# A four-stage sandwich on one core: weight loads issued in the first block, the convolution written a group ahead, gate and router products moved into the norm blocks, bias loops with transposes a group ahead

## The reference, cut to what matters

```python
x = x + ln(conv_attention_mixture(ln(x)))   # stage a
x = x + ln(fp4_experts(ln(x)))              # stage b
x = x + ln(linear_attention(ln(x)))         # stage c
x = x + ln(windowed_transformer(ln(x)))     # stage d, six layers
# stage a
y = xp[:, 0:T]*w_dw[:, 0] + xp[:, 1:T+1]*w_dw[:, 1] + xp[:, 2:T+2]*w_dw[:, 2]
x = x + einsum('btd,ed->bte', y, w_pw)
...                                          # causal linear attention, then
h = ln(x)*ln_g + ln_b
gw = softmax(einsum('btd,ed->bte', h, w_moe_gate))       # 4 experts
ffn = sum_e gw_e * (silu(h @ w1_e.T + b1_e) @ w2_e.T + b2_e)
# stage b
logits = x @ router_w.T                                  # 16 experts, the best 2 kept
out = sum_e combine_e * (expert_e(x) + bias_down_e)
```

## Time and profile before

| what | value |
|---|---|
| median of 3 runs | 5442.13 us (5440.97 to 5442.73) |
| the profiled execution | 5434.87 us, its span 5433.2 us |
| busy: PE, DVE, ACT, POOL | 89%, 74%, 70%, 45% of the span |
| mean granted clock of TensorE | 0.94 of 2.4 GHz |
| blocks from the start to `al` | 94.85 us |
| from the end of `al` to `ax` | 87.88 us |
| from the end of `ax` to `be` | 107.94 us |
| stage d and the output | 4103.20 us |

### The profile page before, as it was taken

How to read it: one execution, slowest core, us unless ns; L and a number is a source line. 1 busy time by engine, 2 the same in 40 slices (tenths; PEclk the granted TensorE clock), 3 DMA queues, 4 the chain that set the end, 5 groups by cost and what they waited for, 6 DMA issues and landing times. The chain is left out here.

```text
span 5433.2 us, 144088 instructions
## 1 busy us (share of the span) xinstructions
PE 4847.8 (89%) x42260; PEld 4060.2 (75%) x42260; DVE 4003.2 (74%) x11109; ACT 3810.0 (70%) x12437; POOL 2451.6 (45%) x3763
## 2 busy tenths in 40 slices
PE   5988949994299998999989998899989999799994
PEld 3657949984188876888778887788867888688883
DVE  5664757777588876888768887788867888688875
ACT  1334423431199986999869997799968999599982
POOL 0000000000466663666546664566636666366661
PEclk7997959997699998999999999999999999999997
DMA  0001100000111111111111111111111111111111
GB/s 21 2 17 39 39 1 0 0 0 4 49 27 27 27 49 27 27 27 27 51 28 27 27 27 47 29 27 27 27 50 28 27 27 27 51 24 27 27 49 31
DMA packets 103390, 149.33 MB, mean 27 GB/s; under 512 B 65245, under 2 KB 72690, under 8 KB 102386
## 3 DMA queue, kind: packets, MB, share of 16 engines
q1 hardware_dynamic: 93410, 107.27, 8.7%
q0 software_dynamic: 9232, 33.12, 1.9%
HBM read 49.13 MB, written 2.10 MB: 9 GB/s over the span
## 5 line engine op out<-in xcount | busy, mean ns | idle before, releaser
L2023 ACT ACTIVATE d_probs<-d_S_ps,d_neg_max 128x96 f32<-128x96 f32 x3072 | 1000.6, 342 | 13.5 <-DVE d_neg_max L2237 3.8
L1626 POOL TENSOR_TENSOR d_qk<-d_qk,d_sin_terms 128x512 f32<-128x512 f32 x768 | 960.8, 1272 | 29.7 <-DVE d_sin_terms L2209 29.7
L1801 PEld LDWEIGHTS d_S_ps<-d_kT,d_q_blocks 128*128 128x128 f32 x6144 | 791.8, 193 | 2.3
L1801 PE MATMUL d_S_ps<-d_kT,d_q_blocks 128*128 128x96 f32 x6144 | 791.1, 272 | 0.0
L2209 DVE TENSOR_TENSOR d_qk<-d_A_ps,d_tables 128x512 f32<-128x512 f32 x768 | 527.6, 687 | 229.0 <-ACT d_squares L1979 162.6
L2023 ACT ACTIVATION_READ_ACCUMULATOR d_probs<-d_S_ps,d_neg_max 128x1 f32 x3072 | 639.3, 208 | 0.0
L1758 PE MATMUL d_A_ps<-d_wqkv_hi,d_xT_hi 128*128 128x512 f32 x1152 | 556.2, 483 | 22.1 <-DVE d_sin_terms L2209 17.4
L1979 ACT ACTIVATE d_squares<-d_A_ps 128x512 f32<-128x512 f32 x768 | 462.6, 602 | 123.9 <-PE d_A_ps L1760 123.5
L2209 DVE TENSOR_TENSOR d_sin_terms<-d_A_ps,d_tables 128x512 f32<-128x512 f32 x768 | 522.8, 681 | 0.0
L1765 PE MATMUL d_T_ps<-d_ident,d_qk 128*128 128x128 f32 x3072 | 483.9, 281 | 36.5 <-POOL d_qk L1663 32.8
L2031 ACT ACTIVATE d_probsT<-d_PT_ps 96x512 f32<-96x512 f32 (+1 forms) x768 | 459.9, 599 | 79.8 <-PE d_PT_ps L1811 79.6
(11 more groups left out here) (406 smaller groups left out, 10766.6 us busy)
## 6 DMA issues: line engine op xcount, KB each, us to landing
d_v_early<-d_v SPq DMA_DIRECT2D x192, 256.0 KB, 3.0
d_v_early<-d_v SPq DMA_DIRECT2D x192, 128.0 KB, 2.3
d_tables<-L_ffn_rotary POOLq DMA_DIRECT2D x7, 2048.0 KB, 8.3
d_qk<-L_ffn_Wqkv POOLq DMA_DIRECT2D x21, 512.0 KB, 3.9
d_xs<-d_xb SPq DMA_DIRECT2D x56, 127.0 KB
d_xs<-d_xb SPq DMA_DIRECT2D x96, 63.5 KB
ax_fp_blocks<-L_ffn_blocks_gu SPq DMA_DIRECT2D x16, 256.0 KB, 3.7
ax_fp_scales<-L_ffn_scales_gu SPq DMA_DIRECT2D x64, 64.0 KB, 3.0
```

Of the source, the lines that this page charges most:

```text
L1626: nc.gpsimd.tensor_tensor(c4[:, :, s, :], c4[:, :, s, :], s4[:, :, 1 - s, :], ALU.add).then_inc(rotated, 1)
L1801: last = nc.tensor.matmul(S[g % 2][:, n * SEEN:(n + 1) * SEEN], qx[:, p, half, :], kT[b][jj][:, p, HALF * half:HALF * half + SEEN], start= ...
L2023: nc.scalar.activation(pr[:, g, n, seen_columns(g)], S[g % 2][:, n * SEEN:(n + 1) * SEEN], ACT.Exp, bias=nmax[:, g, n:n + 1], accum_out=de ...
```

## The change

- The first block and the block of six loads are gone. A function `load` runs on SP inside the `an` norm: x in eight transfers (a quarter of both halves each, with a semaphore for each quarter), then the identity, the ten weights of `av` and the six arrays of the gate and experts. DVE waits for a quarter ahead of each 8 tiles of statistics. The loads of `bt` are issued inside the norm `bn`.
- ACT copies a whole group of 4 transposed tiles in one instruction in all four norms.
- In `ao` and `bn` PE computes the logits of group g-1 behind the transposes of group g.
- `av` is written out without a loop. ACT makes the first tap, DVE the other two, one group ahead of the additions.
- In `as` and `bt` PE transposes group g+1 ahead of the product of group g. In `as` the softmax comes first, and the high and low parts are made between the groups of the loop. In `bt` DVE does the copy to y in ACT's place, and the high and low parts go into the loop in eighths.

The loads and the norm:

```diff
+            def load(sp):
+                x4 = x[:].rearrange("p (j b) d -> p j b d", b=B)
+                for q in range(4):
+                    js = slice(4 * q, 4 * q + 4)
+                    for b in range(B):
+                        sp.dma_start(x4[:, js, b, :], x_from[b].rearrange("(j p) d -> p j d", p=P)[:, js, :]).then_inc(x_in[q], DMA)
+                sp.dma_start(ident[:], ident_from).then_inc(ident_in, DMA)
...
             for n in range(N_TILES):
+                if arrived is not None:
+                    v.wait_ge(arrived[n // 8], 2 * DMA)
                 nc.vector.bn_stats(stats[:, n, :], x[:, n, :]).then_inc(stat, 1)
...
+            def project(g):
+                out, weight, columns, done = logits
+                pe.wait_ge(T_out, g + 1)
+                for t in range(G4):
+                    n = G4 * g + t
+                    last = nc.tensor.matmul(out[:, n * columns:(n + 1) * columns], xT(g)[:, t, :], weight, start=True, stop=True)
+                last.then_inc(done, 1)
...
                 last.then_inc(T_ps, 1)
+                if logits is not None and g:
+                    project(g - 1)
+            if logits is not None:
+                project(GROUPS - 1)
```

The convolution:

```diff
+                    for g in range(GROUPS):
+                        if g >= 2:
+                            act.wait_ge(t_ps, g - 1)
+                        nc.scalar.activation(cv[:, g % 2], taken(g, 0), ACT.Identity, scale=wdw[:, 0:1]).then_inc(tap, 1)
...
+                    def convolve(g):
+                        v.wait_ge(tap, g + 1)
+                        for k in (1, 2):
+                            if k == 2:
+                                v.wait_ge(conv, 2 * g + 1)
+                            nc.vector.scalar_tensor_tensor(cv[:, g % 2], taken(g, k), wdw[:, k:k + 1], cv[:, g % 2], ALU.mult, ALU.add
+                                                           ).then_inc(conv, 1)
...
+                    convolve(0)
+                    for g in range(GROUPS):
+                        if g < GROUPS - 1:
+                            convolve(g + 1)
+                        v.wait_ge(d_ps, g + 1)
```

The bias loop of `as` (that of `bt` is changed alike):

```diff
+                        pe.wait_ge(mixed, 1)
+                        transpose_mix(0)
+                        for g in range(GROUPS):
+                            if g < GROUPS - 1:
+                                transpose_mix(g + 1)
                             pe.wait_ge(gT_out, g + 1)
+                            if g >= 2:
+                                pe.wait_ge(y_out, g - 1)
                             for t in range(G4):
                                 last = nc.tensor.matmul(yb[g % 2][:, t * D:(t + 1) * D], gT[:, G4 * g + t, :], b2[:], start=True, stop=True)
                             last.then_inc(y_ps, 1)
```

More of the change, by code:

```diff
@@ L111, in normalise_rows, with _ @@
     with nc.Block() as block:
+        if load is not None:
+            @block.sync
+            def _(sp):
+                load(sp)
         @block.vector
@@ L142, in _ @@
                 last.then_inc(T_ps, 1)
+                if logits is not None and g:
+                    project(g - 1)
+            if logits is not None:
+                project(GROUPS - 1)
         @block.scalar
         def _(act):
+            if scale is not None:
+                act.wait_ge(weights_in[0], weights_in[1])
             for g in range(GROUPS):
                 act.wait_ge(T_ps, g + 1)
[L148 to L154, removed]
+                dst, src = xT(g), banks[g % 4][:].rearrange("p (t k) -> p t k", k=P)
+                if len(dst.shape) == 4:
+                    src = banks[g % 4][:].rearrange("p (t b k) -> p t b k", b=B, k=P)
+                if scale is None:
+                    ins = nc.scalar.activation(dst, src, ACT.Copy)
+                else:
+                    ins = nc.scalar.activation(dst, src, ACT.Identity, scale=scale, bias=bias)
+                ins.then_inc(T_out, 1)
 def add_normalised(nc, ctx, tag, x, y):
@@ L563, in conv_attention_mixture @@
         x1 = m.sb("x1", [P, N_TILES, D])
+        gb = m.sb("ln_g_b", [P, 2])
+        w1 = m.sb("w1", [P, AE * AF])
+        wm = m.sb("w_moe_gate", [P, AE])
+        b2 = m.sb("b2", [AE, D])
+        w2 = m.sb("w2", [P, AE * AC, D])
+        b1 = m.sb("b1", [P, AE * AC])
+        conv_in, moe_in, ident_in = m.sem("conv_in"), m.sem("moe_in"), m.sem("ident_in")
+        x_in = [m.sem(f"x_in{q}") for q in range(4)]
         with ExitStack() as c1:
@@ L588, in conv_attention_mixture, with taken @@
                 tb = [m2.bank("x1_0"), m2.bank("x1_1")]
-                loaded, zeroed, conv, d_ps, t_ps, d_out, t_out, first = (
-                    m2.sem(s) for s in ("loaded", "zeroed", "conv", "d_ps", "t_ps", "d_out", "t_out", "first"))
+                zeroed, tap, conv, d_ps, t_ps, d_out, t_out, first = (
+                    m2.sem(s) for s in ("zeroed", "tap", "conv", "d_ps", "t_ps", "d_out", "t_out", "first"))
+                def taken(g, k):
+                    return xc[:, :, g * (2 * P) + k:(g + 1) * (2 * P) + k]
@@ L1035, in conv_attention_mixture, with _, transpose_mix @@
                     hTf = hT[:].rearrange("p n t -> p (n t)")
+                    @block.sync
+                    def _(sp):
+                        sp.wait_ge(moe_in, 6 * DMA)
                     @block.tensor
                     def _(pe):
-                        for n in range(N_TILES):
-                            last = nc.tensor.matmul(lb[:, n * AE:(n + 1) * AE], hT[:, n, :], wm[:], start=True, stop=True)
-                        last.then_inc(lg_ps, 1)
-                        pe.wait_ge(mixed, 1)
-                        for g in range(GROUPS):
+                        def transpose_mix(g):
                             if g >= 2:
                                 pe.wait_ge(gT_out, g - 1)
-                                pe.wait_ge(y_out, g - 1)
                             for t in range(G4):
```

210 lines of the change are left out of this document (103 added, 107 removed).

## The result

The changed kernel takes 5355.3 us (median of four runs, 5351.5 to 5359.0), the kernel before 5441.6 beside it: ratio 0.9836, 95% interval 0.9824 to 0.9848, some 86 us less. The profiled execution took 5351.48 us in place of 5434.87, its span is 5349.4 in place of 5433.2. The forecast was 5369, the range 5335 to 5386: faster as said. Between the two profiled executions it is 83.4 us, 10 more than the sum of 73.2.

What follows compares the result with a forecast made beforehand. No one engine bounds the kernel; engines take turns, so the chain from event to event counts. The terms sum to 73.2 us, taken from the median 5442.1: 5369 us; own range 5358 to 5384, stated range 5335 to 5386.

Steps and rivals of the forecast that it cites:

- rival 1: Packed norms and bias loops run at the high clock: 32 us more gained together, 5337 us; chance 0.22.
- x in quarters: First norm's statistics work while x lands, ending near 12.6 in place of 17.9: 5.3 us gained.
- copies: One ACT copy where four stood behind the last transposes of `an` and `cn`: 0.4 us gained together.
- Convolution: Convolution block: next taps ready for PE, no wait for weights; 30.7 us gained, bounds 27.4 to 33.0.
- Block of loads: Ahead of the norm `ao`, DVE's 9.63 us wait shrinks to an ordinary change of blocks: 9.3 us gained.
- Logits inside the norms: Norms `ao` and `bn`: PE bounds them with 2.75 us a group; 4.0 and 3.4 us gained.
- Softmax first: Gate's softmax in `as`: maximum to first transpose takes 2.1 us in place of 8.4; 6.3 us gained.
- Bias loops: Loops of `as` and `bt`: transposes ahead hide ACT's copy, a group takes 2.82 us; 6.9 us gained each.
- Rival 2: Start of the kernel: weights are served beside x, statistics end at 22.6, total 5379 us; chance 0.08.
- Rival 3: Convolution still goes in turns, a group near 6.5 us, 24 of the 30.7 lost, 5393 us; chance 0.03.
- Rival 4: Linear attention runs at the low clock throughout, costing 122 us: slower, 5491 us; chance 0.02.
- Rival 5: Change gives nothing, savings come back as waits in the experts' blocks, 5440 us; chance 0.03.

Runs made afterwards that it cites:

- the wide kernels: The changed kernel with logits padded to 128 columns, 5341.6 us; with bias loops at 128 rows and columns, 5329.9 us; with both, 5328.6 us.

## Why the prediction was right, and where it was off

The way and most of the size came as forecast, and nine of ten stretches lie within some 2 us of their terms. But 5355.3 us lies below the forecast's own range (5358 to 5384) and below 5361, what all its terms at their bounds would give. It is inside the stated 5335 to 5386 only because I had stretched that downwards for rival 1, which did not come. That part was luck.

- *x in quarters*, 5.3, and *copies*, 0.2 of the 0.4: 5.64 measured. Right, and shown by making the statistics wait for all of x.
- *Convolution*, 30.7: 36.6 measured, above my upper bound of 33.0. This is the term that was most off. The step that failed is the size of DVE's work for a group, "1.65 + 2 x 0.69 + some 0.1 of waits = 3.1": the two taps take 1.53 when nothing makes the second wait long, each operation starts a little before the one ahead is done, and the group is 2.65. Also I took the mean between a low and a high clock, and it rose behind the first group. By my own numbers the high clock alone was 24.8 for eight groups in place of 27, 2.2; the 0.45 that I had too much for a group is 8 x 0.45 = 3.6. Together 5.8 of the 5.9.
- *Block of loads*, 9.3: 9.27 (the wait fell to 0.36). The 0.14 that is missing in the table is the linear attention.
- *Logits inside the norms*, 4.0 and 3.4: 5.8 and 5.6, above both bounds (5.3 and 4.7). The pace was 2.45 us and not 2.75: a change between transposes and logits costs nothing, and products issued one behind the other take 1.57 from start to start, not 1.72. The clock stayed low as forecast. What I did not see is that the packing itself, compared with logits behind the transposes, loses 2.9 us in each norm. Nor was DVE the bound of all of `ao`, as I had it: its end was set by ACT's 32 copies, 4.6 us behind the last transpose. The sum was right all the same, since it went from event to event.
- *Softmax first*, 6.3: 6.29, confirmed by its undoing (6.8, of which 0.5 is the high parts' new place).
- *Bias loops*, 6.9 each: 6.35 and 6.27, from a group of 2.95 and not 2.82: the four transposes take 0.95 between two products, where I took 0.85 of them. Confirmed by their undoing (6.4 each).
- *Clock and rival 1.* The clock was 0.50 in all four places, as forecast, and rival 1 did not come. My reading, that narrow products don't raise it, was an inference from two windows of a PE that had stood idle ahead; the wide kernels show it for these places. The Trainium skill ("TensorE: Matmul & The Clock Gate", Part 1) ties the clock to how busy PE has been; these runs disagree for products of 4 or 16 columns and for products of 4 or 16 rows, busy 16.00 of 16.00 us in the norm `ao` and 20.00 of 20.00 in each loop at 0.50, and agree once the same work fills the array. The price that I gave the rival (32 us) was about right in sum: the two widenings gained 6.7, 8.8, 6.8 and 9.5, 31.8 in all, less than my 8.4 in the norms and more than my 6.6 and 8.4 in the loops.
- *Rival 2*, the weights crowd x, false: the statistics ended at 12.24 to 12.54 us in profiles with the weights behind x and at 12.27 without. *Rival 3* false. *Rival 4*, the low clock kept throughout the linear attention, did not come, but it has a small form that I had not priced: a late rise, 6.4 us. *Rival 5* false.
- Not in the sum: 1.2 us in the experts of stage a. Profiles with the same code there took 234.6 to 236.2 us, against 235.25 and 236.46, so this may be spread.
- Three sums of the prediction are off by a little: the norm's parts add up to 22.3 and not 22.2, with switches of 0.22 to 24.0 and not 24.5, and the terms at their upper bounds to 81.5 and not 81.2. None of this changes the forecast.

## What to carry to other kernels

Look for chains in which two engines take turns, and write the next group's work ahead of the wait: what that gives can be read from one group of the timeline, here within a fifth for the convolution and a tenth for the loops. When an engine goes from waiting to bounding, cost it by start-to-start times, not by durations with waits between. Look also at the engine that only copies: its lag behind the last product can set the end of a block. Ask of any PE work with few rows or columns at which clock it runs: here padding it to 128 was worth 32 us, while packing it among the transposes lost 2.9 us in each norm.

## What was not expected of the hardware

- A product of 128 columns ran faster than one of 4 (1.06 against 1.71 us for four tiles), because it let the clock rise; 64 passes of 4 columns even lost a clock of 1.00 that they had been handed, with PE busy 5.00 of 5.00 us.
- The clock rose 12 or 26 us into the same code, entered at the same time, 6.4 us apart in the end.
- A loop of DVE lost 3.5 us at each of its seven returns, and 41 us with what hung on it, when the first taps of the convolution stood ahead of it in DVE's program, and nothing when 57 empty instructions were added to these. Some instructions more in an early block can thus cost more in a late one than they take themselves.
